# A mixture-of-experts kernel: rows gathered seven tiles ahead instead of five, their weights kept in a ring of four

## The reference

```
x = x + tanh(g_xattn) * scan_block(ctx_1024, layernorm(x))
h = layernorm(x)                                   # 2048 tokens x 512
scores = softmax(h @ gate_w.T)                     # 16 experts
topk_w, topk_ids = top_k(scores, 6);  topk_w /= topk_w.sum()
out = sum over the experts e of  c_e * (silu(h @ w1_e.T) * (h @ w3_e.T)) @ w2_e.T      # I = 352
out = out + swiglu(h, sw13, sw2)                   # the shared expert, twice as wide
x = x + tanh(g_ffn) * out
```

## Time and profile before

| | |
|---|---|
| median of 3 runs | 1468.71 us (1467.18 to 1472.8) |
| profiled execution | 1467.74 us, its span 1466.0 us |
| TensorE busy | 1324.9 us, 90% of the span |
| GpSimd busy | 942.5 us, 64% |
| VectorE busy | 830.4 us, 57% |
| ScalarE busy | 730.6 us, 50% |

### The profile page before, as it was taken

One profiled execution on the slowest core, in us unless ns is written; L12 is line 12 of the kernel. 1 busy time (PEld: TensorE's weight loads), 2 busy tenths in 40 slices (PEclk: granted clock), 3 DMA queues, 4 the chain that ended last, 5 costly groups with the idle time before them and its releaser, 6 DMA issues.

```text
span 1466.0 us, 30647 instructions
## 1 busy us (share of the span) xinstructions
PE 1324.9 (90%) x8064; PEld 1191.3 (81%) x8065; DVE 830.4 (57%) x1468; ACT 730.6 (50%) x1317; POOL 942.5 (64%) x671
## 2 busy tenths in 40 slices
PE   6897988998888899999789888998999988898996
PEld 3776877888888899999789788987888888898895
DVE  6888897988998755742344434343344343443341
ACT  5899897897888353433233333332333233333331
POOL 0599898998898577885554666455655665536632
PEclk8899999998999999999899999999999999999998
DMA  4111122131242554665676777777776776767763
GB/s 134 43 68 33 56 88 101 38 130 54 62 150 70 152 131 85 140 141 94 186 214 156 205 195 202 198 170 197 194 204 163 188 207 193 216 160 199 198 161 44
DMA packets 136275, 205.90 MB, mean 140 GB/s; under 512 B 20496, under 2 KB 74384, under 8 KB 134016
## 3 DMA queue, kind: packets, MB, share of 16 engines
q1 hardware_dynamic: 101744, 102.33, 23.2%
q0 software_dynamic: 31024, 62.10, 22.5%
q10 hardware_dynamic: 3440, 40.63, 7.7%
HBM read 130.99 MB, written 76.25 MB: 141 GB/s over the span
## 4 chain that ended last, share of the span: by engine, by line
PE 41%; DMA 15%; issue 6%; DVE 3%; POOL 3%; POOLq 1%; ACT 1%; SPq 0%; DVEq 0%; ACTq 0%
PE bank L1794 15%; PE bank L1774 11%; PE bank L1775 11%; DMA xs<-token_quarters 10%; DMA xt<-token_rows,gid 5%; PE bank L1785 2%; DVE hs L1233 1%; POOL w L1043 1%; PE bank L1684 1%; PE bank L1670 1%; POOLq L1088 1%; ACT ys L924 1%; DVE al L1475 1%; POOL out_x L1071 1%; PE bank L1682 0%
## 5 line engine op out<-in xcount | busy, mean ns | idle before, releaser
L1005 POOL TENSOR_TENSOR hc<-hs,crow 128x512 f32<-128x512 f32 x254 | 322.3, 1305 | 90.0 <-DVE hs L1233 84.5
L1774 PE MATMUL bank<-w,xh 128*128 (+1 forms) x1088 | 364.2, 336 | 1.4 <-issue 1.2
L1071 POOL DMA_INDIRECT out_x<-ys,aid x104 | 165.3, 1589 | 307.4 <-issue 287.4
L1775 PE MATMUL bank<-w,xh 128*128 (+1 forms) x1088 | 352.3, 324 | 0.0
L1794 PE MATMUL bank<-w,ah 128*128 (+1 forms) x816 | 274.7, 419 | 66.9 <-DVE al L1475 66.8
L1233 DVE TENSOR_TENSOR_SCAN hs<-dA,bank 128x512 f32<-128x512 f32 x256 | 295.7, 1208 | 50.5 <-PE bank L1684 30.5
L1794 PEld LDWEIGHTS bank<-w,ah 128*128 128x128 f32 x816 | 157.3, 199 | 103.6 <-issue 76.7
L924 ACT COPY ys<-bank 128x512 f32<-128x512 f32 x136 | 79.9, 587 | 282.5 <-PE bank L1794 282.5
L1774 PEld LDWEIGHTS bank<-w,xh 128*128 128x128 f32 x1088 | 206.4, 190 | 9.4 <-issue 1.6
L1775 PEld LDWEIGHTS bank<-w,xh 128*128 128x128 f32 x1088 | 207.9, 191 | 5.9
L1475 DVE TENSOR_TENSOR al<-bank,ah 128x384 fp32r<-128x384 f32 x136 | 75.0, 552 | 234.0 <-ACT ah L918 229.4
(11 more groups left out here) (183 smaller groups left out, 1999.9 us busy)
## 6 DMA issues: line engine op xcount, KB each, us to landing
raws<-in_wall ACTq DMA_DIRECT2D x16, 2176.0 KB, 8.7
token_quarters<-xt SPq DMA_DIRECT2D x104, 256.0 KB
xs<-token_quarters SPq DMA_DIRECT2D x104, 256.0 KB, 3.7
crow<-c_rows SPq DMA_DIRECT2D x64, 256.0 KB, 3.3
xt<-token_rows_turned SPq DMA_DIRECT2D x32, 256.0 KB, 3.2
out_x<-ys POOLq DMA_DIRECT2D x32, 256.0 KB, 4.3
token_rows<-rowb SPq DMA_DIRECT2D x4, 1028.0 KB, 6.0
xrow<-in_x SPq DMA_DIRECT2D x4, 1024.0 KB, 8.0
```

What stands on the lines that cost most here:

```text
L1005: nc.gpsimd.tensor_tensor(hc[:, j, :], hs[:, j, :], crow[:, n % 4, :], ALU.mult).then_inc(hc_done, 1)
L1071: pool.indirect_dma_start(out_rows, bass.IndirectOffsetOnAxis(ap=aid[:, s:s + 1], axis=0), ys[:, s, :], None, bounds_check=TOKENS - 1, oob ...
L1774: nc.tensor.matmul(gate_bank[:, 0:I], xx, columns(w, off + ww + k * 2 * I, I), start=first, stop=last)
L1775: mm = nc.tensor.matmul(up_bank[:, 0:I], xx, columns(w, off + ww + k * 2 * I + I, I), start=first, stop=last)
```

## The change

Gathers run seven tiles ahead (`AHEAD`), so VectorE prepares `gid` for tile t+7 in tile t. Since a gather into `xt[T % 4]` needs the weights of T-4 out of it, these are now taken three tiles ahead (`TAKEN`), into a ring of four `cc` columns instead of two. `gid[T % 4]` is overwritten earlier too, so a new copy `keep_ids` holds the row numbers in `mid` until `add_ids` moves them on to `aid`. The first gathers start one shared tile earlier (tile 28, `NS - 4`), and with them the wait for the lists; weights are taken from shared tile 29 on. VectorE's last four tiles are written out behind its loop, as they have nothing left to gather.

```diff
-AHEAD = 5
-FIRST_ROWS = {NS - 3: (NS, NS + 1), NS - 2: (NS + 2,), NS - 1: (NS + 3, NS + 4)}
+AHEAD = 7
+TAKEN = AHEAD - 4
+FIRST_ROWS = {NS - 4: (NS,), NS - 3: (NS + 1,), NS - 2: (NS + 2, NS + 3), NS - 1: (NS + 4, NS + 5, NS + 6)}
...
-        cc = alloc(ctx, "cc", [P, 2])
+        cc = alloc(ctx, "cc", [P, 4])
...
+        mid = alloc(ctx, "mid", [P, 4], I32)
...
-                if t == NS - 3:
+                if t == NS - 4:
                     pool.wait_ge(wts_stored, 16 * NB)
                     pool.wait_ge(rows_stored, 16 * (NB + 1))
...
-                at_least(dve, am_done, t - 1)
-                nc.vector.tensor_copy(cc[:, s4 % 2:s4 % 2 + 1], xt[:, s4, bass.ds(H - 1 + number, 1)]).then_inc(cc_done, 1)
+                at_least(dve, am_done, t - 3)
+                nc.vector.tensor_copy(cc[:, s4:s4 + 1], xt[:, s4, bass.ds(H - 1 + number, 1)]).then_inc(cc_done, 1)
...
+            def keep_ids(t, s4):
+
+                apart(dve, gid_done, t + 1, "dve")
+                apart(dve, aid_done, t - 3, "dve")
+                nc.vector.tensor_copy(mid[:, s4:s4 + 1], gid[:, s4:s4 + 1]).then_inc(mid_done, 1)
+
             def add_ids(t, s4):
 
-                apart(dve, gid_done, t + 1, "dve")
+                apart(dve, mid_done, t + 1, "dve")
                 apart(dve, added[s4], through(t - 4, s4), "dve")
-                nc.vector.tensor_copy(aid[:, s4:s4 + 1], gid[:, s4:s4 + 1]).then_inc(aid_done, 1)
+                nc.vector.tensor_copy(aid[:, s4:s4 + 1], mid[:, s4:s4 + 1]).then_inc(aid_done, 1)
...
+                if takes and not plain:
+                    take_weight(t + TAKEN, slot_of(TAKEN), number, group_of(TAKEN))
+                    keep_ids(t + TAKEN, slot_of(TAKEN))
+                if not static or t + 1 >= NS:
+                    add_ids(t + 1, slot_of(1))
+                if static and t < NS:
                     for late in FIRST_ROWS.get(t, ()):
+                        if late >= NS + 4:
+                            dve.wait_ge(mid_done, late - 3)
                         gather_ids(late, late % 4)
...
+                elif gathers:
+                    apart(dve, mid_done, t + TAKEN + 1, "dve")
+                    gather_ids(t + AHEAD, slot_of(AHEAD), column)
...
             for t in range(1, PEELED):
-                if t == NS - 3:
+                if t == NS - 4:
                     dve.wait_ge(ids_in, 16)
```

More of the change, by code:

```diff
@@ L473, in mamba_moe @@
         aid_done = sem("aid_done")
+        mid_done = sem("mid_done")
         ids_in = sem("ids_in")
@@ L1419, in fill_table @@
                 n = NT - AHEAD
-                chained(nc.vector.scalar_tensor_tensor(out=packed[:, 0:n], in0=meta[:, 0, 1:n + 1], scalar=float(NX), in1=meta[:, 2, 0:n],
+                chained(nc.vector.scalar_tensor_tensor(out=packed[:, 0:n], in0=meta[:, 0, TAKEN:n + TAKEN], scalar=float(NX), in1=meta[:, 2, 0:n],
                                                        op0=ALU.mult, op1=ALU.add))
@@ L1453, in gather_ids, with multiply @@
                 nc.vector.tensor_copy(gid[:, s4:s4 + 1], lists[:, bass.ds(ids_column(t) if column is None else column, 1)]).then_inc(gid_done, 1)
+            def keep_ids(t, s4):
+                apart(dve, gid_done, t + 1, "dve")
+                apart(dve, aid_done, t - 3, "dve")
+                nc.vector.tensor_copy(mid[:, s4:s4 + 1], gid[:, s4:s4 + 1]).then_inc(mid_done, 1)
             def add_ids(t, s4):
-                apart(dve, gid_done, t + 1, "dve")
+                apart(dve, mid_done, t + 1, "dve")
                 apart(dve, added[s4], through(t - 4, s4), "dve")
-                nc.vector.tensor_copy(aid[:, s4:s4 + 1], gid[:, s4:s4 + 1]).then_inc(aid_done, 1)
-            def multiply(t, s):
+                nc.vector.tensor_copy(aid[:, s4:s4 + 1], mid[:, s4:s4 + 1]).then_inc(aid_done, 1)
+            def multiply(t, s4):
+                s = s4 % 2
                 dve.wait_ge(sg_done, t + 1)
@@ L1466, in multiply @@
                     dve.wait_ge(cc_done, t + 1)
-                    weight = cc[:, s:s + 1]
+                    weight = cc[:, s4:s4 + 1]
                 at_least(dve, am_turned, t - 1)
@@ L1522, in beside, with tile, slot_of, group_of @@
                         fill_table(i)
[L1524 to L1527, removed]
-                    beside(DVE_AFTER_A, t)
+            def tile(t, place, m=None, takes=True, gathers=True):
+                def slot_of(d):
+                    return (place + d) % 4
+                def group_of(d):
+                    return None if m is None else m + (place + d) // 4
+                s, static = place % 2, isinstance(t, int)
+                plain = static and t + TAKEN < NS
+                if not plain:
+                    split, number, column = plan_of(t)
+                if not static or t + 1 >= NS:
+                    turn(t + 1, slot_of(1), group_of(1))
+                a_low(t - 1, 1 - s)
+                if static:
+                    beside(DVE_AFTER_A, t)
+                if takes and not plain:
+                    take_weight(t + TAKEN, slot_of(TAKEN), number, group_of(TAKEN))
+                    keep_ids(t + TAKEN, slot_of(TAKEN))
+                if not static or t + 1 >= NS:
+                    add_ids(t + 1, slot_of(1))
+                if static and t < NS:
@@ L1546, in tile @@
                 x_low(t + 1, 1 - s)
-                multiply(t, s)
-                next_weights(t, split)
+                multiply(t, place % 4)
+                if not static or t >= PEELED:
+                    next_weights(t, split)
             dve.sem_inc(cc_done, NS)
@@ L1566, in _ @@
             for t in range(1, PEELED):
-                if t == NS - 3:
+                if t == NS - 4:
                     dve.wait_ge(ids_in, 16)
+                    dve.sem_inc(mid_done, NS)
                     dve.sem_inc(gid_done, NS)
@@ L1573, in _ @@
             dve.wait_ge(meta_ready, 2)
[L1574 to L1579, removed]
+            for t in range(PEELED, NS + 3):
+                tile(t, t % 4)
+            looped = dve.value_load(fours[0:1, 2:3], min_val=E // 4 - 2, max_val=ROUTED // 4 - 2)
+            with dve.Fori(0, looped) as i:
                 for k in range(4):
-                    tile(4 * i + NS + 3 + k, (3 + k) % 4, True, i + 1)
+                    tile(4 * i + NS + 3 + k, 3 + k, i)
             last = tiles_but_12(dve) + 11
+            for k in range(4):
+                tile(last - 4 + k, 3 + k, looped, k < 2, False)
             a_low(last - 1, 0)
-            multiply(last, 1)
+            multiply(last, 3)
             a_low(last, 1)
```

## The result

The median after is 1421.36 us (1420.27 to 1426.68, four runs) against 1467.95 of before (1466.72 to 1472.8, four runs): a ratio of 0.9684, 95% interval 0.965 to 0.9717. The profiled execution took 1422.3 us, its span is 1420.5.

A forecast was written before the change was run, and what follows sets the result against it. TensorE's stalls behind late rows at experts' starts were taken as the removable cost: 1467.7 us less 73.7 for stalls, plus 21 for the add and 5 for the first tiles, gives 1420 us; range 1398 to 1450.

The forecast's parts named there:

- The stalls (-73.7): Routed loop, r2 to r100: TensorE's stalls behind late rows, 5.3 us per expert, all go; bounds 0 and 73.7.
- Rival 3: Put and set stay slow beside the weight load; only about 1 us per expert goes: 1459 us, chance 0.09.
- SP's waits for gathers nearly vanish: Sign to look for in SP's loop: its 559.9 us of waits for gathers in 97 waits nearly disappear.
- The forecast of 25 and of 18 us: Routed tiles: put can leave 25 us before its tile's transpose; 18 us are left for the set.
- The wait for the add (+21): At an expert's start VectorE's aid waits 2.3 us for a late add; TensorE idles 1.4, for 15 experts.
- Rival 1: The add costs nothing, landing in time or covered by VectorE's slack: 1399 us, chance 0.16.
- Rival 2: The new idle takes TensorE's clock down, 52 us in place of 21: 1451 us, chance 0.18.
- The first routed tiles (+5): From tile 28 on: list wait, new stalls and slow clock against first-row waits that go; net +5, bounds -5 and +12.
- The three stalls: VectorE's waits for weights in tiles 29, 30 and 31: 2.7, 0.5 and 4.6 us, with 3.2 of slow clock.
- The copy mid (0): VectorE's extra 128x1 copy per routed tile, about 0.3 us, is covered before TensorE's matmul: 0; uncovered 31 us.
- rival 4: The mid copy waits for GpSimd's subtraction, as the skill's lock rule would give: 153 us more, 1552 us, chance 0.03.

The follow-up runs named there:

- small_low: The kernel before, with GpSimd subtracting only 16 of 4352 values per partition for the next expert's low half: 1462.82 us, ratio 0.9952.
- small_weights: The kernel before, with weight loads in the loop bringing 16 of 4352 values a partition: 1461.68 us, ratio 0.9942.
- aid_late: The kernel after, with VectorE's copy to aid behind multiply(t) instead of ahead of xl: 1394.07 us, ratio 0.9477.
- ahead5: The kernel after, gathering five tiles ahead as before, with mid, the ring of four weights and the rewritten loop kept: 1469.22 us, ratio 0.9997.

## Why the prediction was right

1420 us was forecast and 1421.36 came. That close an agreement is in part luck: for the stalls and the add together -52.7 was forecast and -49.1 came from r2 to r100, for the first tiles +5 and +3.0, and +1.4 came ahead of the change. The steps, one by one:

**The stalls (-73.7): right in size, incomplete in cause.** All of them went: the excess of 33.6 is 9.0 for the starts and 24.6 for the new wait. The prediction gave one story, a set that is late already and then slow beside the weights. The runs show two causes that cover each other: the slow set (small_low keeps the whole stall) and the gather behind the subtraction (small_weights keeps 37.1 us of waits for al, and adds 22.0 for xl). Rival 3 priced the second at "about 1 us per expert"; with the weight loads cut it is 2.7 (37.4 us over 14 starts), and with the wait for the add it holds nearly the whole excess. The forecast came out because seven tiles outlast both. Had the change taken away the weight load alone, the same reasoning would have promised some 5% and got 0.6%.

**"SP's waits for gathers nearly vanish": wrong.** They went from 559.9 to 489.0 us. The step that failed is that put(T) would be held by the transpose of T-4: its gather still lands later. Put(r49), for example, leaves at 1009.36 behind a gather of 1005.04 that took 4.1 us, while the transpose of r45 was issued at 1007.30.

```profile
1005.04 0.98 POOL L1056 DMA_INDIRECT xt<-token_rows,gid  x1 [0.30 <-issue]
...
1007.30 0.73 DVE L1432 STREAM_TRANSPOSE bank<-xs 128x512 f32<-128x512 f32 x1 [0.35 <-issue]
...
1009.36 0.36 SPq L670 DMA_DIRECT2D token_quarters<-xt  x1
```

What the change moved is the distance: over 95 tiles the median from put to transpose went from 12.2 to 23.7 us, and from set to transpose from 4.5 to 16.6, never under 11.6. The forecast of 25 and of 18 us for the two was near. SP's wait is the wrong thing to read; the transpose's is the right one.

**The wait for the add (+21): right.** At the start shown it is 14.28 us from the eviction to the add (14.17 forecast), 4.8 to its landing (5.0), aid 2.50 late (2.3), TensorE 1.30 idle (1.4). The step takes 7.86, as against "near 7.7", and the sum is 24.6. Of VectorE's 26 waits ahead of aid, 15 are of 2.0 to 2.7 us; the other eleven, of 0.3 to 1.6, held TensorE once, for 0.35. Rival 1 is out by the xl row. Rival 2 is out by the windows: the clock stood at 1.00 behind the idle spell, and on the mean of the whole loop. aid_late shows the cause.

**The first routed tiles (+5): +3.0, in other parts.** The wait for the lists was bigger, 6.24 us of idle for 5.0 forecast, with the clock at 0.50 behind it as said; in aid_late, the same up to there, it was 4.68, so its size differs from one execution to the next. The three stalls after it were 1.41, 1.92 and 1.73, not 2.7, 0.5 and 4.6, and the clock stayed up, where 3.2 us were set aside. The two errors cancel in part; the mis-sized term is the third stall, and the slow clock set aside for it and the first.

**The copy mid (0): right.** It ran in 0.15 us at 1030.76, in the middle of the 9.61 us subtraction, so rival 4 falls with its 1552 us. The exclusive lock that the Trainium skill states for a VectorE copy in a two-port mode (SBUF — State Buffer, "SBUF: two separate sides") doesn't show on this copy; whether a copy of one element per partition runs in such a mode, no run here shows. ahead5 prices all the bookkeeping together: 0.9997.

## What to carry over

When two delays reach the same wait, taking either away can show almost nothing; before a term is put down to one cause, look in the trace for what would be late next if it were gone. Buffering one tile further ahead was enough here because it outlasts both, and the next wait was then found in the order of one engine: an instruction that waits for a slow DMA belongs behind the work that others need, here one moved copy for another 2%. In a chain of prefetches read the slack at the consumer, not the waits of the queue that feeds it.

## What the hardware showed beyond that

A set of 2.7 us took 8.99 and 9.4 us beside a weight load of 2176 KB, though it was on another queue.

The length of an idle spell didn't settle the clock alone. Spells of 1.30 and 1.92 us kept 1.00. In small_weights two similar spells parted, 2.89 us ahead of the first window here and 2.63 us ahead of the second:

```profile
834.30:837.30 3.00, 2.96 (x14) 2.59 (x15) 2.02 (x5) 0.78 (x3) 0.00 (x0) 1.00 0.80 220
782.20:785.20 3.00, 2.96 (x7) 2.38 (x8) 2.00 (x5) 0.45 (x2) 0.00 (x0) 0.50 0.69 183
```

What parted the two stays open.
